# Two graph blocks on one core: the high-part products of an attention step placed ahead of the scores of the same step

## What is computed

```python
def _gat_layer(x, W, adj):
    proj = x @ W
    Wh, Ws = jnp.split(proj, 2, axis=-1)
    scores = Wh @ Ws.T
    a = jax.nn.softmax(scores, axis=-1) * adj
    out = a @ Wh
    out = out + x
    return jax.nn.leaky_relu(out, NEG_SLOPE)
```

## Time and profile before

| | |
|---|---|
| median of 3 runs | 1556.11 us (1555.24 to 1556.95) |
| the profiled execution | 1556.08 us |
| its span, first to last instruction | 1554.3 us |
| mean granted TensorE clock | 0.997 |
| busy: TensorE / VectorE / ScalarE / GpSimd | 1530.9 / 1134.8 / 1067.8 / 982.8 us |

### The profile page before, as it was taken

The page is one execution under the profiler, slowest core; times in us unless marked ns, Lnnn a source line. Parts: engine busy times, 40 slices in busy tenths (PEclk is TensorE's granted clock), DMA queues, the critical chain, the costliest instruction groups (busy, mean ns, idle before and its releaser), DMA issues.

```text
span 1554.3 us, 34619 instructions
## 1 busy us (share of the span) xinstructions
PE 1530.9 (98%) x12824; PEld 1524.6 (98%) x12824; DVE 1134.8 (73%) x2119; ACT 1067.8 (69%) x2079; POOL 982.8 (63%) x886
## 2 busy tenths in 40 slices
PE   6999999999999999999999999999999999999998
PEld 5999999999999999999999999999999999999998
DVE  7757666676675677777777777867777777777775
ACT  5689899899984566666666666656666666666666
POOL 4312222222210488888888888847888888888885
PEclk9999999999999999999999999999999999999999
DMA  4354444544430134444434435622344334444343
GB/s 159 70 105 127 117 116 121 147 120 117 118 100 28 37 93 106 105 107 106 106 105 107 105 107 164 196 55 83 105 106 106 106 102 104 105 106 106 104 108 109
DMA packets 98423, 166.92 MB, mean 107 GB/s; under 512 B 16079, under 2 KB 29134, under 8 KB 97998
## 3 DMA queue, kind: packets, MB, share of 16 engines
q1 hardware_dynamic: 70208, 116.84, 28.1%
q0 software_dynamic: 24336, 44.31, 11.9%
q10 hardware_dynamic: 3710, 3.56, 0.7%
HBM read 152.05 MB, written 12.62 MB: 106 GB/s over the span
## 4 chain that ended last, share of the span: by engine, by line
PE 93%; DVE 2%; POOL 1%; ACT 1%; issue 1%; DMA 1%; SPq 0%; DVEq 0%; ACTq 0%; POOLq 0%
PE PS L1361 36%; PE PS L1575 9%; PE PS L1577 9%; PE PS L1582 9%; PE PS L1429 5%; PE PS L1438 5%; PE PS L1434 5%; PE PS L1428 5%; PE PS L1433 5%; DMA STGT<-adjt 1%; POOL X L539 1%; POOL FR L546 0%; DMA X<-xt 0%; DVE AF L1168 0%; DVE ROW L905 0%
## 5 line engine op out<-in xcount | busy, mean ns | idle before, releaser
L546 POOL TENSOR_TENSOR FR<-AF,FR 128x512 fp32r<-128x512 f32 x338 | 451.1, 1335 | 117.5 <-ACT FR L757 113.3
L1361 PE MATMUL PS<-FR,RB 128*128 128x256 f32 x3900 | 515.8, 282 | 0.3 <-ACT X L711 0.2
L1361 PEld LDWEIGHTS PS<-FR,RB 128*128 128x128 f32 x3900 | 483.4, 189 | 1.7 <-ACT X L711 1.7
L539 POOL TENSOR_TENSOR X<-X,ROW 128x512 f32<-128x512 f32 x283 | 371.4, 1313 | 78.8 <-ACT ROW L767 78.8
L1575 PE MATMUL PS<-FR,RA 128*128 128x256 f32 x1300 | 326.2, 284 | 0.1
L1577 PE MATMUL PS<-FR,RA 128*128 128x256 f32 x1300 | 321.4, 280 | 0.0
L1168 DVE TENSOR_TENSOR AF<-PS,AJ 128x512 f32<-128x512 f32 x338 | 231.1, 684 | 59.5 <-ACT PS L723 50.0
L711 ACT ACTIVATE X<-PS 128x512 f32<-128x512 f32 x272 | 162.3, 597 | 154.9 <-DVE AF L1100 147.7
L488 POOL DMA_DIRECT2D STGT<-adjt x169 | 90.5, 536 | 279.6 <-PE PS L1438 279.6
L1100 DVE TENSOR_TENSOR AF<-PS,AF 128x512 f32<-128x512 f32 x286 | 196.4, 687 | 94.7 <-PE PS L1361 92.0
L1575 PEld LDWEIGHTS PS<-FR,RA 128*128 128x128 f32 x1300 | 245.0, 188 | 0.2 <-DVE RA L1082 0.2
(11 more groups left out here) (175 smaller groups left out, 2352.4 us busy)
## 6 DMA issues: line engine op xcount, KB each, us to landing
AJ<-adjt SPq DMA_DIRECT2D x338, 256.0 KB, 2.7
STGT<-adjt POOLq DMA_DIRECT2D x169, 256.0 KB, 3.0
xt_scratch<-ROW SPq DMA_DIRECT2D x11, 512.0 KB, 2.6
RB<-xt_scratch SPq DMA_DIRECT2D x11, 512.0 KB, 6.1
x_scratch<-X ACTq DMA_DIRECT2D x13, 256.0 KB, 2.6
ROW<-x_scratch SPq DMA_DIRECT2D x13, 256.0 KB, 3.3
out<-ROW SPq DMA_DIRECT2D x12, 256.0 KB, 3.4
ROW<-rec_scratch SPq DMA_DIRECT2D x23, 128.0 KB, 3.9
```

The costliest lines, as they stand in the source:

```text
L539: nc.gpsimd.tensor_tensor(slot, slot, MB.unsqueeze(1).broadcast_to([P, 2, 256]), ALU.subtract)\
L546: nc.gpsimd.tensor_tensor(LO[g % 2], WA[g % 2], HI[g % 3].bitcast(F32), ALU.subtract)\
L1361: last = nc.tensor.matmul(out, stationary(a, k), moving(b, k), start=(k == 0 and i == 0), stop=(k == K - 1 and i == 2))
```

## The change

`weigh(g)` is cut in two. `weigh_high(g)` keeps the waits at the front, `hi_d` and the eight matmuls with the high part. `weigh_low(g)` keeps `alo_d`, the four matmuls with the low part and the increment of `av_mm`. In each step `weigh_high` stands ahead of `scores`, and `weigh_low` where `weigh` stood. No instruction is added, removed or changed, and no other engine's program is touched.

```diff
-            def weigh(g):
+            def weigh_high(g):
                 b, u = g // UNITS, g % UNITS
...
+            def weigh_low(g):
+                b, u = g // UNITS, g % UNITS
+                tiles = [(2 * u + h, d, h * 256) for h in range(2) for d in range(K)]
                 pe.wait_ge(alo_d, g + 1)
...
                 if S_END.get(v - 1) == PAIRS:
                     turn_max(PAIRS)
+                if a is not None and a < GL:
+                    weigh_high(a)
                 if s is not None:
                     scores(s)
                 if S_END.get(v - 1) not in (None, PAIRS):
...
                 if a is not None and a < GL:
-                    weigh(a)
+                    weigh_low(a)
                 elif a is not None:
                     weigh_last(a)
```

## The result

| | before | changed |
|---|---|---|
| median | 1555.67 us (4 runs, 1554.56 to 1556.95) | 1573.80 us (4 runs, 1573.02 to 1574.08) |
| span of the profiled execution | 1554.3 us | 1571.8 us |
| mean granted clock | 0.997 | 0.999 |

The changed kernel is slower: its time is 1.0115 times that of before (95% interval 1.0102 to 1.0128), 18.1 us more between the medians. 1574.1 was predicted.

What follows compares the result with a forecast made beforehand. TensorE, working without a pause, was taken to set the pace. Turn stalls 15.4 us, plus late high parts 2.9, less 0.3 at the last block, made 18.0 us: 1574.1 us, range 1566 to 1582.

Steps and rivals of the forecast that it cites:

- No step costs anything by itself: All steps: no matmul comes or goes and every wait stays, so the edit in itself costs nothing.
- The turn's stall: At `turn_max_back`, now covered by only four low matmuls: TensorE waits 0.70 us in 22 turns, 15.4 us.
- The odd turn, counted as zero: Turn whose spread VectorE's queue holds up: high products fill the 0.92 us in front of `turn_max`; no loss.
- The high part, needed earlier: `hi_d` needed at the step's start; tightest in the second step behind a turn, margin 0.35 us: no stall.
- The places that were late already: First weighed chunk 1.42 us, second layer's second step 0.87, behind the layer weights' conversion 0.62: together 2.9 us lost.
- The end: Last block's transposes waited 0.6 us in two places; earlier high products can fill half: -0.3 us.
- Sum: Whole kernel: 15.4 + 2.9 - 0.3 = 18.0 us slower, 1574.1 us.
- late high parts in every block: Rival: every block's second step misses its 0.35 us margin; 1587.7 us, or 1581 at half; chance 0.13.
- a paid-back stall: Rival: part of the turn's stall returns, a turn costs 0.35 us; 1566.4 us; chance 0.09.
- not slower: Rival: `turn_max_back` finds its tile ready; within 0.2% of before, or 1553.8 us without early waits; chance 0.05.
- the clock: Rival: TensorE's clock falls at each turn, 22 x 1.5 = 33 us more, 1607 us; chance 0.03.

Runs made afterwards that it cites:

- one: The changed kernel with `turn_max` moved ahead of the scores, behind the high-part products, in the 23 turn steps: 1559.01 us, ratio 1.0023 to before.
- three: New order in the 302 steps outside the turns of the maxima, the 23 turn steps as before: 1558.66 us, ratio 1.0023 to before.
- seven: The kernel before with ScalarE's spread of the maxima done twice, the first into an unread tile: 1560.87 us, ratio 1.0033 to before.
- two: New order only in the 23 steps of a turn of the maxima, all others as before: 1571.23 us, ratio 1.0103 to before.
- twelve: The kernel before with only chunk 321's step, which holds the last scores of all, in the new order: ratio 1.0001 to before.
- four: Order of before, but `turn_max_back` stands between the eight high and four low products of its step: 1560.22 us, ratio 1.0034 to before.
- five: Order of before, but `turn_max_back` stands directly behind `turn_max`, ahead of all twelve products: 1582.81 us, ratio 1.0174 to before.
- ten: The kernel before with only chunks 323 and 324, the two steps ahead of the last block, in the new order: ratio 1.0003 to before.
- nine: The kernel before with only chunks 0, 145, 146, 169, 170, 323 and 324 in the new order: 1557.54 us, ratio 1.0019 to before.
- the table of four points: `turn_max_back`'s mean wait by products between the two transposes: 12 (before) one turn only, 8 (four) 0.23 us, 4 (two) 0.72, 0 (five) 1.20.

## Why the prediction was right, step by step

- *No step costs anything by itself.* Shown by one and three: with the new order in 302 or 325 steps and the turns out of it, 0.23% is left, and their regular blocks of the first layer are as long as before (38.86 us in one, 38.87 in three, 38.88 before).
- *The turn's stall.* The mechanism is shown by all of one to seven. L1639 starts 1.35 us after L1633, for 1.34 predicted, and its load waits 0.70 us (16.0/23). The total loss in a block is less, 0.62 us: the fourth and the fifth turn's L1633 stand at 642.27 and 681.75 after, at 639.19 and 678.05 before, 39.48 and 38.86 us apart. Over all regular blocks but the two longest it is 0.63. In two, where only the turn's steps have the new order, the blocks are 0.72 us longer in the first layer and 0.70 in the second, the whole forecast. So 0.08 us a block come back only where the other steps have the new order too; by which mechanism is not shown.
- *The odd turn, counted as zero.* Wrong in its mechanism: all 23 turns wait, this one too, and no 0.92 us in front of `turn_max` are left to be filled. The VectorE operation that held this turn up, L1115, takes 0.41 us here in the changed kernel. Before, it took 3.42 us, across three GpSimd operations that follow each other without a pause:

```profile
985.32 1.33 POOL L539 TENSOR_TENSOR X<-X,ROW 128x512 f32<-128x512 f32 x1
986.01 3.42 DVE L1115 TENSOR_TENSOR ROW<-AF 128x256 f32<-128x256 f32 x1
986.57 1.33 POOL L546 TENSOR_TENSOR FR<-AF,FR 128x512 fp32r<-128x512 f32 x1
987.82 1.33 POOL L539 TENSOR_TENSOR X<-X,ROW 128x512 f32<-128x512 f32 x1
```

  It is no event of a single execution: at this place it takes 3.4 us in four traces (before, two, seven, twelve), 0.9 in three (four, five, ten) and at most 0.46 in the other seven: the six with the new order in the steps around it, and nine. From the `turn_max_back` ahead of this turn to the one behind it before takes 97.13 us, ten, with the same order there, 95.67, and the changed kernel 97.51. So the profiled execution of before has 1.46 us in it that need not be there, and against it the stretch lost only 0.38 us. I built a term on a thing that comes and goes. With all turns the term is 23 x 0.63 = 14.5 us instead of 22 x 0.70 = 15.4.
- *The high part, needed earlier.* Margin 0.35 predicted, 0.37 measured, no stall. But the steps with a block's result have less than I had looked at. There VectorE waits for the load of the row sums' reciprocals, and at one block of the trace it came late:

```profile
738.29 0.70 DVE L1207 TENSOR_TENSOR PS<-PS,ROW 128x512 f32<-128x512 f32 x1 [0.61 <-DMA ROW<-rec_scratch]
738.90 0.68 DVE L1168 TENSOR_TENSOR AF<-PS,AJ 128x512 f32<-128x512 f32 x1
739.62 0.63 ACT L757 ACTIVATE FR<-AF 128x512 fp32r<-128x512 f32 x1 [1.30 <-DVE AF L1168]
...
740.30 0.38 PE L1575 MATMUL PS<-FR,RA 128*128 128x256 f32 x1
```

  Mask and high part came late with it, and this block is 0.5 us longer than its neighbours. In one's trace a wait of 1.0 us at the same line makes a block 0.9 us longer (40.18 us). The old order covers most of this: before's trace has five such waits of up to 0.5 us, ten's has eight of up to 2.0, and only one of ten's blocks is 0.3 us longer.
- *The places that were late already.* 1.4 us predicted and measured at the first chunk (L1575 waits 1.41 us for L1082). Nine's trace gives 1.41, 0.65 and 0.95 us for the three places, 3.0 together, where 1.42, 0.62 and 0.87 were forecast.
- *The end.* The sign was wrong: -0.3 forecast, about +0.95 measured (72.1 against 71.1 us). Ten, which moves only the two steps ahead of the last block, gains 0.1 us at most (71.0), so there was next to nothing to fill. I looked for waits that the earlier products could fill and forgot that the last scores, which come later, start the chain to the end.
- *Sum.* 14.5 + 3.0 + 0.95 = 18.4 us; 18.1 measured between the medians, with some 2 us of interval. Between the two profiled spans it is 17.5: the late reciprocals add 0.5 there, the 1.46 us of the odd turn in the trace of before go off, and what is left is within 0.1 us, partly because smaller differences (the attention starts 0.5 us earlier in the trace after) cancel. The forecast of 18.0 owes some of its exactness to such luck: a stall that was too large, an odd turn left out and an end of the wrong sign made up for each other.

Of the rivals, late high parts in every block fell by the margin of 0.37 us, a paid-back stall by the table of four points, "not slower" by L1639's 23 waits. For the clock: it stays at 1.00 in the long stretch in spite of 11 idle times of about 0.5 to 0.7 us. The stretch at half speed of the earlier trace rows stands behind a longer one, 2.02 us in front of TensorE's product at 490.50.

## What to carry to other kernels

In this stream without pauses, the new order had no price of its own in an ordinary step. Look, for every wait, at how much of the engine's own work stands between the instruction that starts the chain and the one that waits for its end. Compare that with the chain's length, from a place where the helpers visibly idle. When work is moved out of such a pair, move the start of the chain ahead with it: here `turn_max` ahead of the scores gives back four fifths of the loss. And ask which moved instruction is the last of its kind, since the tail of a stage hangs on it.

## What I had not expected

A VectorE operation on two columns took 0.82 us in place of 0.17, from 1518.74 to 1519.56, while GpSimd's L539 ran from 1518.23 to 1519.54. The Trainium skill (SBUF — State Buffer, "SBUF: two separate sides") says that VectorE, in some of its modes, and GpSimd share a pair of ports as an exclusive lock, and the second to come is blocked until the first is done. The trace agrees with it here, and L1115 fits too. Before, it begins inside a GpSimd operation, two more follow without a pause, and it ends at 989.43, 0.28 us behind the end of the third. In ten it begins inside one and ends 0.27 us behind the end of that one, and the next GpSimd operation takes 1.48 us in place of 1.30. In the changed kernel it begins just behind the end of one and takes 0.41 us. So the order of TensorE's work seems to decide whether the two meet, by when it lets VectorE begin; no run here changed this alone.
